# Layer 1 of a two-layer cross-attention model: the DMA transposes issued by ScalarE instead of SyncE, and VectorE's reciprocals ahead of the scaling of x

## The chip, the cores and the metric

The kernel runs on one core of a Trainium2 chip. The metric is the device time in microseconds (us) of one execution. The time before is the median of three runs, 813.28 us.

## The reference, cut to what matters

Two layers work on x of 32 blocks (batches) of 128 rows by 128 columns. Layer 0 is a cross-attention of 16 heads of 8 columns and a routed feed-forward block of 8 experts. The change touches only layer 1, for each block:

```python
def _act_quant(x):
    scale = 127.0 / jnp.clip(jnp.max(jnp.abs(x), axis=-1, keepdims=True), 1e-05)
    xq = jnp.clip(jnp.round(x * scale), -128.0, 127.0) / scale

# attention of layer 1: 16 heads of 64 columns, one null key and value beside the 128 of the context
sim = jnp.einsum('bhid,bhjd->bhij', q * scale, k)
attn = jax.nn.softmax(sim, axis=-1)
out = jnp.einsum('bhij,bhjd->bhid', attn, v)
out = _ln(out @ Wo, lno_s, lno_b)

# feed-forward of layer 1, with weights rounded to -1, 0, 1 and activations rounded to 8 bits
gate = jax.nn.silu(_bitlinear(x, w_gate))
up = _bitlinear(x, w_up)
return _bitlinear(gate * up, w_down)
```

## The kernel before, in words

Every engine has an instruction list of its own, written out by hand, and the engines are held together by semaphores alone. An engine takes its list strictly in order, so an instruction that waits holds back all that stand behind it. This holds for the queues that issue DMAs too: SyncE's (SP) list consists of waits and DMA issues.

Layer 0 ends at about 345 us. Then the loop of layer 1 runs over b = 0 to 31, one pass for each block, in `attention_ffn_block`. In pass b the attention of block b is computed, while the queries, keys and first score product of block b + 1 are made ready, the output projection and norm of earlier blocks are finished, and the feed-forward part of block f = b - 3 is worked on. A pass of the loop stands in the lists of all engines:

- TensorE (`tensor_part`): scores of b, queries of b + 1 (L1807), values of b (L1849), keys of b + 1 (L1819), the gate product of f (`gate_part`, L1953), the down product of f - 1 (`down`, L1988), the up product of f (L1964), the weighted values of b (L1915), the sums of the exponentials (`sums`, L1926 and L1928), the output projection of b - 1 (L1834), and small products with the row maxima (L1892, L1902). `gate_part(f)` writes the bank `pb`, which held half of the values of block b, so it waits until ScalarE has copied those out: `pe.wait_ge(v_ready, 2 * (f + 3) + 1)`.
- ScalarE (`scalar_part`): exponentials of half a block (`exps`, L2090), copies of queries (L2115), of row maxima (L2094), of values (`v_copy`, L2120), the tanh (L2126), the second exponentials, more copies, the scaling of h (L2133), and as the last of a pass `maxima_copy(b + 1, 0)` (L2094).
- VectorE (`vector_part`): row maxima, norms, the product of the attention output with the reciprocals (`normalise`, L2252, twice), and at the end of a pass `multiply(f)` (L2317), `h_range(f)` (L2323 to L2328), `quantise_x(b - 2)` (six instructions, L2292 to L2305, that end in `xq`, the rounded x in bf16), and `inverse(b)` (L2243), the reciprocals `rT` of the sums.
- GpSimd (`pool_part`): gathers, small norms, and the rounding of h to `hq` (`hidden_round`, L1583).
- SyncE (`sync_part`): stores and loads, and two chains. The first spreads the reciprocals over the partitions through DRAM: `store_reciprocals(b)` (L1474, `a_r_rows<-a_rT`), which waits for `inverse(b)`, and then `spread(b)`, four DMAs (L1483, `a_r_all<-a_r_rows`), which wait for the landing of the first. `normalise(b)`, in VectorE's next pass, waits for them. The second chain turns `xq` and `hq` by DMA transposes: `turn_x(b - 2)` (L1462, `f_xqT<-f_xq`) and `turn_h(b - 3)` (L1467, `f_hqT<-f_hq`), whose results `gate_part` and `down` use in the next pass.

The order in SyncE's list is what ties these together:

```python
            if 2 <= b < LAST + 2:
                turn_x(b - 2)
            if b + 1 < B:
                store_reciprocals(b)
            if 3 <= b < H_LAST + 3:
                turn_h(b - 3)
            if b + 1 < B:
                spread(b)
```

Of the kernel before, what the change touches and what calls it, by code (L numbers as in the profile page):

```python
# [18 lines left out]
def wait(eng, sem, value):  # L19

    if isinstance(value, int) and value <= 0:
        return
    eng.wait_ge(sem, value)
# [1256 lines left out]
def attention_ffn_block(nc, ctx, consts, w, wff, early, x_res, psum, before, gathered, out):  # L1280
# [3 lines left out]
    B, S, D, F = 32, P, P, 512  # L1284
    FC = F // P
# [98 lines left out]
    LAST = B - 3  # L1384
# [6 lines left out]
    H_LAST = LAST - 1  # L1391
# [58 lines left out]
    def sync_part(sp):  # L1450
        def context(b):
            sp.wait_ge(xcn_ready, b - 1)
            sp.dma_start(cin[:, b % 2, :], w["ctx"][b]).then_inc(cin_ld[b % 2], 16)

        def store(f):
            sp.wait_ge(x4_ready, f + 1)
            sp.dma_start(out[f], x4[:, f % 2, :]).then_inc(stored[f % 2], 16)

        def turn_x(f):
            sp.wait_ge(xq_ready, f + 1)  # L1460
            wait(sp, up_done, f)
            sp.dma_start_transpose(xqT[:].unsqueeze(1), xq[:]).then_inc(xq_in, 16)  # L1462

        def turn_h(f):
            sp.wait_ge(hq_ready, f + 1)
            wait(sp, down_done, f)
            sp.dma_start_transpose(hqT[:].rearrange("p (c q) -> p c q", c=FC), hq[:]).then_inc(hq_in, 16)  # L1467

        def store_reciprocals(b):
            sp.wait_ge(inverse_seq, b + 1)  # L1470
            if b >= 1:
                for half in range(2):
                    sp.wait_ge(r_spread[half], 32 * b)
            sp.dma_start(r_rows, rT[0:P:G, :]).then_inc(r_stored, 16)  # L1474

        def spread(b):
            sp.wait_ge(r_stored, 16 * (b + 1))
            if b >= 1:
                sp.wait_ge(oT_ready, 2 * b)
            for half in range(2):  # L1480
                for e in range(2):
                    rows = r_rows.rearrange("(a e i) q -> a e (i q)", a=2, e=2)[half, e]
                    sp.dma_start(r_all[e * HD:(e + 1) * HD, half, :], rows.partition_broadcast(HD)).then_inc(r_spread[half], 16)  # L1483

        context(2)
        context(3)
        for b in range(B):
            if b >= 4:
                store(b - 4)
            if 1 <= b and b + 3 < B:  # L1490
                context(b + 3)
            if 2 <= b < LAST + 2:
                turn_x(b - 2)
            if b + 1 < B:
                store_reciprocals(b)
            if 3 <= b < H_LAST + 3:
                turn_h(b - 3)
            if b + 1 < B:
                spread(b)
        for f in range(B - 4, B):  # L1500
            store(f)
        for s in range(2):
            sp.wait_ge(stored[s], 16 * (B // 2))
# [562 lines left out]
    def scalar_part(act):  # L2066
        act.wait_ge(w_in, N_W)
        act.wait_ge(setup_done, 4)

        def xc_copy(b):  # L2070
            act.wait_ge(tr_done, b + 1)
            wait(act, q_done, 2 * (b - 1))
            nc.scalar.activation(xT[:, b % 2, :], xcp[b][:, 0:S], ACT.Identity, bias=b1[:], scale=s1[:]).then_inc(xT_ready, 1)  # L2073
            if b >= 2:
                wait(act, cTm_ready, b)
                nc.scalar.activation(cT[:], xcp[b][:, S:2 * S], ACT.Identity, bias=1.0, scale=1.0).then_inc(cT_ready, 1)

        def xq_copy(f):
            act.wait_ge(xqt_done, f - LAST + 1)
            wait(act, up_done, f)  # L2080
            nc.scalar.copy(xqT[:], xtp[f]).then_inc(xqT_ready, 1)

        def exps(b, half):
            act.wait_ge(t_done, 2 * b + half + 1)
            for e in range(2):
                if half == 0:
                    wait(act, sums_done, b)
                else:
                    wait(act, pv_done, 2 * b)
                nc.scalar.activation(pT[:, 2 * half + e, :], tp[e], ACT.Exp, scale=SCALE).then_inc(exp_ready, 1)  # L2090

        def maxima_copy(b, half):
            act.wait_ge(row_done, 2 * b + half + 1)
            nc.scalar.copy(mxT[:, half, :], (pb, maxp[1])[half][:, 2 * S:3 * S]).then_inc(row_ready, 1)  # L2094

        def reciprocal_copy(half):
            act.wait_ge(row_done, 2 * B + half + 1)
            if half == 0:
                act.wait_ge(oT_ready, 2 * (B - 1))
            nc.scalar.copy(r_all[:, half, :], r_bank[half]).then_inc(row_ready, 1)  # L2100

        def null_exp(b):
            act.wait_ge(row_ready, 2 * b + 2)
            wait(act, sums_done, b)
            nc.scalar.activation(pnT[:], mxT[:, 1, :], ACT.Exp, scale=SCALE).then_inc(pn_ready, 1)

        def k_copy(b):
            act.wait_ge(k_done, 2 * b + 2)
            wait(act, t_done, 2 * (b - 1))
            nc.scalar.copy(kT[:, b % 2, 4:8, :].rearrange("p n k -> p (n k)"), key_bank(b, 1)).then_inc(kT_ready[1], 1)  # L2110

        def q_copy(b, half):
            act.wait_ge(q_done, 2 * b + half + 1)
            wait(act, t_done, 2 * (b - 1))
            nc.scalar.copy(qT[:, b % 2, 4 * half:4 * half + 4, :].rearrange("p n q -> p (n q)"), (pa, pb)[half]).then_inc(qT_ready, 1)  # L2115

        def v_copy(b, half):
            act.wait_ge(v_done, 2 * b + half + 1)
            wait(act, pv_done, 2 * (b - 1))
            nc.scalar.copy(v[:, b % 2, 8 * half:8 * half + 8, :].rearrange("p h d -> p (h d)"), value_bank(b, half)).then_inc(v_ready, 1)  # L2120

        def gate_tanh(f):
            act.wait_ge(gate_done, f + 1)
            act.wait_ge(sg_ready, 2 * f + 2)
            wait(act, gt_ready, f)
            nc.scalar.activation(th[:], gate_of[f], ACT.Tanh, scale=sgh[:, f % 2:f % 2 + 1]).then_inc(th_ready, 1)  # L2126

        def h_scale(f):
            act.wait_ge(hr_ready, f + 1)
            if f == 0:  # L2130
                act.wait_ge(p_set, 3)
            wait(act, hq_ready, f)
            nc.scalar.activation(ht[:], h[:], ACT.Identity, scale=hr[:], bias=big_m[:]).then_inc(ht_ready, 1)  # L2133

        def h_copy(f):
            act.wait_ge(htr_done, f - H_LAST + 1)
            wait(act, down_done, f)
            nc.scalar.copy(hqT[:], htp[f]).then_inc(hqT_ready, 1)

        for b in range(2):  # L2140
            v_copy(b, 0)
            v_copy(b, 1)
        xc_copy(0)
        q_copy(0, 0)
        q_copy(0, 1)
        maxima_copy(0, 0)
        for b in range(B):
            more = b + 1 < B
            f = b - 3 if b >= 3 else None
            if b == 0:  # L2150
                xc_copy(1)
            exps(b, 0)
            if more:
                q_copy(b + 1, 0)
            maxima_copy(b, 1)
            if b >= 2:
                v_copy(b, 0)
            if f is not None:
                gate_tanh(f)
            null_exp(b)  # L2160
            exps(b, 1)
            if b >= 2:
                v_copy(b, 1)
            if more:
                q_copy(b + 1, 1)
            if f is not None:
                h_scale(f)
            if b >= 1 and more:
                k_copy(b + 1)
            if b + 2 < B:  # L2170
                xc_copy(b + 2)
            if not more:
                break
            maxima_copy(b + 1, 0)
        f = LAST
        xq_copy(f)
        reciprocal_copy(0)
        reciprocal_copy(1)
        h_copy(f - 1)
        gate_tanh(f)  # L2180
        xq_copy(f + 1)
        gate_tanh(f + 1)
        h_scale(f)
        xq_copy(f + 2)
        gate_tanh(f + 2)
        h_copy(f)
        h_scale(f + 1)
        h_scale(f + 2)
        h_copy(f + 1)
        h_copy(f + 2)  # L2190

    def vector_part(dve):
# [46 lines left out]
        def inverse(b):  # L2239
            dve.wait_ge(sums_done, b + 1)  # L2240
            if b >= 1:
                dve.wait_ge(r_stored, 16 * b)
            nc.vector.reciprocal(rT[:], denP).then_inc(inverse_seq, 1)  # L2243
# [107 lines left out]
        for b in range(B):  # L2351
# [22 lines left out]
            if f is not None:  # L2374
                multiply(f)
                h_range(f)
            if b >= 2:
                quantise_x(b - 2)
            inverse(b)
            if b < 3:  # L2380
                weight_signs(b)
        f = LAST
# [147 lines left out]
```

## Time and profile before

| | us |
|---|---|
| median of three runs | 813.28 |
| lowest and highest | 813.21, 814.16 |
| the profiled execution, its own time | 821.97 |
| its span, first to last instruction | 820.2 |
| busy in the span: TensorE matmul | 775.9 (95%) |
| VectorE | 661.5 (81%) |
| GpSimd | 479.6 (58%) |
| ScalarE | 436.1 (53%) |

The granted TensorE clock is 0.975 of full speed over the span, and 1.00 in every stretch of layer 1 from 360 to 800 us. A busy share is the time in which at least one instruction of the engine ran, as a share of the span. Issuing a DMA isn't counted as busy; the profile lists such issues under SPq for SyncE's queue and ACTq for ScalarE's. Weight loads of TensorE stand apart as PEld and overlap the matmuls.

### The profile page before, as it was taken

The numbers are of one execution on the slowest core, as the hardware profiler recorded it, in microseconds if no ns is written. First come the engines' busy times: TensorE is split into PE (matmuls) and PEld (weight loads), VectorE is DVE, ScalarE is ACT, GpSimd is POOL, SyncE is SP. The second block draws the span as 40 slices with busy tenths as digits, with TensorE's granted clock in tenths as the row PEclk, the third lists the DMA queues.
The fourth block names the chain that finished last, engine by engine and source line by source line (L and its number), as shares of the span: only waits on it lengthen the run. The fifth ranks groups of instructions, "written<-read, shape, count | busy, mean of one in ns | idle before, by whom it ended". The sixth has DMA issues, their size and how long they took to land.

```text
span 820.2 us, 28896 instructions
## 1 busy us (share of the span) xinstructions
PE 775.9 (95%) x10878; PEld 655.3 (80%) x10908; DVE 661.5 (81%) x1747; ACT 436.1 (53%) x1049; POOL 479.6 (58%) x912
## 2 busy tenths in 40 slices
PE   8999999998898997999999999999999999999983
PEld 6777777776698996888888888888888888888861
DVE  6888989877756664578889888888898888988876
ACT  4666666656065773445455554554554545545542
POOL 7767678887856773335554654654655646555234
PEclk9999999989999999999999999999999999999995
DMA  8986220000421211112132231231221222213110
GB/s 245 374 331 255 102 86 15 16 21 28 142 72 49 64 50 36 38 50 64 48 77 57 54 81 47 54 82 46 67 69 48 81 52 55 81 48 76 42 39 14
DMA packets 72892, 66.76 MB, mean 81 GB/s; under 512 B 28354, under 2 KB 53682, under 8 KB 72754
## 3 DMA queue, kind: packets, MB, share of 16 engines
q1 hardware_dynamic: 57890, 40.66, 18.0%
q10 hardware_dynamic: 12816, 20.06, 6.6%
q0 software_dynamic: 2048, 4.20, 1.7%
q8 instruction: 87, 1.43, 0.7%
q14 instruction: 51, 0.42, 0.2%
HBM read 35.89 MB, written 24.37 MB: 73 GB/s over the span
## 4 chain that ended last, share of the span: by engine, by line
PE 49%; DVE 22%; SPq 11%; DMA 10%; issue 5%; ACT 1%; POOL 1%; DVEq 1%; another core or an unknown queue 0%; POOLq 0%; ACTq 0%
DMA a_r_all<-a_r_rows 7%; SPq L1483 4%; PE psum L1039 4%; PE psum L432 4%; PE psum L421 3%; DVE a_mxf L2231 3%; PE psum L1027 3%; PE psum L414 3%; PE psum L1807 3%; SPq L1462 3%; PE psum L1915 3%; PE psum L1881 2%; SPq L1467 2%; PE psum L1834 2%; DVE f_h L2317 2%
## 5 line engine op out<-in xcount | busy, mean ns | idle before, releaser
L2090 ACT ACTIVATE a_pT<-psum 128x512 f32<-128x512 f32 x128 | 69.5, 594 | 63.4 <-PE psum L1902 41.1
L1589 POOL TENSOR_TENSOR f_hd<-f_hmc,a_wmean 128x1 f32<-128x1 f32 x32 | 6.8, 212 | 135.5 <-DVE f_hr L2328 134.3
L720 DVE TENSOR_REDUCE l_mx<-psum 128x4 bf16<-128x512 f32 x128 | 81.8, 681 | 4.5 <-PE psum L403 2.9
L2231 DVE TENSOR_REDUCE a_mxf<-psum 128x8 f32<-128x1024 f32 x64 | 77.5, 1210 | 5.3 <-PE psum L1871 5.3
L1807 PEld LDWEIGHTS psum<-a_xT,a_Wq 128*128 128x128 f32 x512 | 66.5, 197 | 18.2 <-issue 14.1
L1819 PEld LDWEIGHTS psum<-a_cTm,a_Wk 128*128 128x128 f32 x512 | 64.3, 192 | 13.9 <-issue 13.9
L552 ACT ACTIVATE l_pT<-psum 128x512 f32<-128x512 f32 x128 | 70.6, 597 | 8.5 <-PE psum L421 8.2
L1807 PE MATMUL psum<-a_xT,a_Wq 128*128 128x128 f32 x512 | 73.2, 288 | 0.6 <-ACT a_xT L2073 0.6
L1583 POOL TENSOR_SCALAR f_hq<-f_ht 128x512 bf16<-128x512 f32 x31 | 60.4, 1947 | 19.9 <-ACT f_ht L2133 19.8
L1881 PE MATMUL psum<-a_qT,a_kT 64*128 64x128 f32 x1024 | 71.5, 280 | 0.0
L1849 PE MATMUL psum<-a_Wv,a_cTm 128*128 128x512 f32 x128 | 69.7, 630 | 0.0
L1819 PE MATMUL psum<-a_cTm,a_Wk 128*128 128x128 f32 x512 | 67.1, 275 | 0.0
L2133 ACT ACTIVATE f_ht<-f_h,f_big_m,f_hr 128x512 f32<-128x512 f32 x32 | 26.0, 814 | 72.2 <-DVE f_hr L2328 70.0
L1915 PE MATMUL psum<-a_pT,a_v 128*32 128x128 f32 x2048 | 63.0, 274 | 0.3 <-DVE a_oT L2252 0.3
L1881 PEld LDWEIGHTS psum<-a_qT,a_kT 64*128 64x128 f32 x1024 | 62.5, 189 | 0.0
L1834 PE MATMUL psum<-a_Wo,a_oT 128*128 128x128 f32 x512 | 62.5, 275 | 0.0
L1915 PEld LDWEIGHTS psum<-a_pT,a_v 128*32 128x32 f32 x2048 | 53.7, 110 | 9.0 <-issue 7.0
L1834 PEld LDWEIGHTS psum<-a_Wo,a_oT 128*128 128x128 f32 x512 | 59.7, 192 | 0.0
L421 PEld LDWEIGHTS psum<-negI,l_mx 128*128 128x128 bf16 x512 | 35.3, 100 | 25.6 <-DVE l_mx L720 22.7
L2252 DVE TENSOR_TENSOR a_oT<-psum,a_r_all 128x512 f32<-128x512 f32 x64 | 41.9, 680 | 9.1 <-issue 5.9
L1100 ACT ACTIVATE e_hT<-psum,e_w1t 128x128 f32<-128x128 f32 x156 | 44.6, 369 | 6.5 <-issue 5.9
L2120 ACT COPY a_v<-psum 128x512 f32<-128x512 f32 x64 | 37.6, 587 | 18.7 <-PE psum L1849 18.7
(315 smaller groups left out, 2075.4 us busy)
## 6 DMA issues: line engine op xcount, KB each, us to landing
sorted_x<-r_zeros ACTq DMA_DIRECT2D x12, 1408.0 KB, 6.9
a_r_all<-a_r_rows SPq DMA_DIRECT2D x124, 128.0 KB
e_xt<-sorted_x SPq DMA_DIRECT2D x39, 64.0 KB, 1.8
sorted_y<-e_yt ACTq DMA_DIRECT2D x39, 64.0 KB, 1.6
e_w<-in_E_W1b SPq DMA_DIRECT2D x1, 2064.0 KB
a_cin<-in_ctx SPq DMA_DIRECT2D x32, 64.0 KB, 2.5
out<-f_x SPq DMA_DIRECT2D x32, 64.0 KB, 2.2
x_res<-in_x SPq DMA_DIRECT2D x1, 512.0 KB, 5.6
```

The lines of the kernel that those rows point to most:

```text
L421: last = nc.tensor.matmul(tp[k][:, j * S:(j + 1) * S], mx[:, b % 2, h:h + 1].to_broadcast([P, P]), negI[:], start=False, stop=(j == Q4 - 1 ...
L552: nc.scalar.activation(pT[:, k, :], tp[k], ACT.Exp, scale=SCALE).then_inc(exp_ready, 1)
L720: nc.vector.tensor_reduce(mx[:, s, Q4 * k:Q4 * k + Q4], maxp[k % 2].rearrange("p (h t) -> p h t", h=Q4), AX_X, ALU.max).then_inc(mx_ready, 1)
L1583: nc.gpsimd.tensor_scalar(hq[:], ht[:], -M, 127.0, ALU.add, ALU.min).then_inc(hq_ready, 1)
L1807: last = nc.tensor.matmul(bank[:, i * S:(i + 1) * S], Wq[:, 4 * half + i, :], xT[:, b % 2, :], start=True, stop=True)
L1819: last = nc.tensor.matmul(bank[:, i * S:(i + 1) * S], Wk[:, 4 * half + i, :], cTm[:, b % 2, :], start=True, stop=True)
L1834: last = nc.tensor.matmul(pa[:, 0:D], oT[:, p, :], Wo[:, p, :], start=(p == 0), stop=(p == NP - 1))
L1849: nc.tensor.matmul(bank, cTm[:, b % 2, :], Wv[:, 512 * half:512 * half + 512], start=True, stop=True).then_inc(v_done, 1)
L1881: last = nc.tensor.matmul(tp[e][:, i * S:(i + 1) * S], kT[r, b % 2, p, :], qT[r, b % 2, p, :], start=(half == 0 and i == 0), stop=(half == ...
L1915: last = nc.tensor.matmul(op[half][32 * j:32 * j + 32, i * S:(i + 1) * S], v[:, b % 2, 8 * half + 4 * e + i, part], pT[:, 2 * half + e, i ...
L2090: nc.scalar.activation(pT[:, 2 * half + e, :], tp[e], ACT.Exp, scale=SCALE).then_inc(exp_ready, 1)
L2231: nc.vector.tensor_reduce(mxf[:, 8 * half:8 * half + 8].rearrange("p (e h) -> p e h", e=2), psum[:, 0:2, :].rearrange("p e (h t) -> p e h ...
```

## The change

`turn_x` and `turn_h` move from SyncE's list into ScalarE's, with the same waits and the same DMAs. In ScalarE's pass they stand at the end, behind `maxima_copy(b + 1, 0)` and ahead of the next pass's `exps(b + 1, 0)`. In VectorE's pass `inverse(b)` moves ahead of `quantise_x(b - 2)`. Nothing is added or taken away.

```diff
@@ sync_part
-        def turn_x(f):
-            sp.wait_ge(xq_ready, f + 1)
-            wait(sp, up_done, f)
-            sp.dma_start_transpose(xqT[:].unsqueeze(1), xq[:]).then_inc(xq_in, 16)
-
-        def turn_h(f):
-            sp.wait_ge(hq_ready, f + 1)
-            wait(sp, down_done, f)
-            sp.dma_start_transpose(hqT[:].rearrange("p (c q) -> p c q", c=FC), hq[:]).then_inc(hq_in, 16)
...
-            if 2 <= b < LAST + 2:
-                turn_x(b - 2)
             if b + 1 < B:
                 store_reciprocals(b)
-            if 3 <= b < H_LAST + 3:
-                turn_h(b - 3)
-            if b + 1 < B:
                 spread(b)
@@ scalar_part
+        def turn_x(f):
+            act.wait_ge(xq_ready, f + 1)
+            wait(act, up_done, f)
+            act.dma_start_transpose(xqT[:].unsqueeze(1), xq[:]).then_inc(xq_in, 16)
+
+        def turn_h(f):
+            act.wait_ge(hq_ready, f + 1)
+            wait(act, down_done, f)
+            act.dma_start_transpose(hqT[:].rearrange("p (c q) -> p c q", c=FC), hq[:]).then_inc(hq_in, 16)
...
             maxima_copy(b + 1, 0)
+            if b >= 2:
+                turn_x(b - 2)
+            if f is not None:
+                turn_h(f)
@@ vector_part
                 multiply(f)
                 h_range(f)
+            inverse(b)
             if b >= 2:
                 quantise_x(b - 2)
-            inverse(b)
```

ScalarE's list from the scaling of h (`f_ht`) at the end of one pass to the copy of the values (`a_v`) in the next. Before:

```order
L2133 ACTIVATE f_ht<-f_h,f_big_m,f_hr 128x512
L2110 COPY a_kT<-psum 128x512
L2073 ACTIVATE a_xT<-psum,a_b,a_s 128x128
L2076 ACTIVATE a_cT<-psum 128x128
L2094 CAST a_mxT<-psum 128x128
L2090 ACTIVATE a_pT<-psum 128x512 x2
L2115 COPY a_qT<-psum 128x512
L2094 CAST a_mxT<-psum 128x128
L2120 COPY a_v<-psum 128x512
```

and with the change:

```order
L2128 ACTIVATE f_ht<-f_h,f_big_m,f_hr 128x512
L2105 COPY a_kT<-psum 128x512
L2058 ACTIVATE a_xT<-psum,a_b,a_s 128x128
L2061 ACTIVATE a_cT<-psum 128x128
L2089 CAST a_mxT<-psum 128x128
L2071 DMA_TRANSPOSE f_xqT<-f_xq 128x1x128
L2076 DMA_TRANSPOSE f_hqT<-f_hq 128x4x128
L2085 ACTIVATE a_pT<-psum 128x512 x2
L2110 COPY a_qT<-psum 128x512
L2089 CAST a_mxT<-psum 128x128
L2115 COPY a_v<-psum 128x512
```

The two transposes now stand between the copy of the row maxima (`a_mxT`) and the exponentials (`a_pT`).

VectorE's list at the end of a pass, from the reciprocal of h's range (`f_hr`) to the copy of the output projection (`a_o`). Before:

```order
L2328 RECIPROCAL f_hr<-f_hmc 128x1
L2292 TENSOR_SCALAR f_xn<-x_res,a_ag,f_rs 128x128
L2294 TENSOR_REDUCE f_am<-f_xn 128x1
L2297 TENSOR_SCALAR f_amc<-f_am 128x1
L2299 RECIPROCAL f_rc<-f_amc 128x1
L2301 TENSOR_SCALAR f_xt<-f_xn,f_rc 128x128
L2305 TENSOR_SCALAR f_xq<-f_xt 128x128
L2243 RECIPROCAL a_rT<-psum 128x128
L2258 TENSOR_TENSOR a_o<-psum,a_null_out 128x128
```

and with the change:

```order
L2327 RECIPROCAL f_hr<-f_hmc 128x1
L2242 RECIPROCAL a_rT<-psum 128x128
L2291 TENSOR_SCALAR f_xn<-x_res,a_ag,f_rs 128x128
L2293 TENSOR_REDUCE f_am<-f_xn 128x1
L2296 TENSOR_SCALAR f_amc<-f_am 128x1
L2298 RECIPROCAL f_rc<-f_amc 128x1
L2300 TENSOR_SCALAR f_xt<-f_xn,f_rc 128x128
L2304 TENSOR_SCALAR f_xq<-f_xt 128x128
L2257 TENSOR_TENSOR a_o<-psum,a_null_out 128x128
```

The reciprocals `a_rT` have moved ahead of the six instructions that make `f_xq`.

## Rows read from the trace of the kernel before

**Rows 1.** Busy time by stretch: length, then each engine's busy us (instructions), clock, DMA.
```profile
core 0: us, PE busy (x) PEld busy (x) DVE busy (x) ACT busy (x) POOL busy (x), PEclk, DMA share, GB/s
617.91:632.61 14.70, 14.61 (x225) 12.68 (x225) 13.08 (x36) 7.73 (x17) 8.02 (x17) 1.00 0.23 64
632.61:647.31 14.70, 14.61 (x225) 12.68 (x226) 12.93 (x36) 7.73 (x17) 8.01 (x17) 1.00 0.22 64
647.31:662.05 14.74, 14.65 (x226) 12.72 (x226) 13.06 (x35) 7.77 (x17) 8.01 (x17) 1.00 0.22 62
543.07:559.00 15.93, 15.47 (x229) 12.94 (x229) 13.16 (x35) 7.68 (x17) 8.04 (x17) 1.00 0.24 59
...
379.40:779.80 400.40, 395.74 (x6017) 341.88 (x6043) 352.50 (x913) 208.70 (x432) 210.76 (x425) 1.00 0.24 62
```
**Rows 2.** Waits from 380 to 780 us: total, times, longest.
```profile
PEld psum L1871 <- DVE a_rT L2243: 2.2, 5, 0.6
DVE a_oT L2252 <- DMA a_r_all<-a_r_rows: 1.4, 3, 0.7
PEld psum L1915 <- DVE a_oT L2252: 1.4, 4, 0.6
```
**Rows 3.** Timeline of SyncE's queue in the pass from 543.07 us: start, us.
```profile
545.05 2.20 SPq L1467 DMA_TRANSPOSE f_hqT<-f_hq  x1
547.93 3.03 SPq L1483 DMA_DIRECT2D a_r_all<-a_r_rows  x4
```
**Rows 4.** Timeline of VectorE around the end of the pass at 632.61 us.
```profile
630.64 0.16 DVE L2328 RECIPROCAL f_hr<-f_hmc 128x1 f32<-128x1 f32 x1
630.72 0.33 DVE L2292 TENSOR_SCALAR f_xn<-x_res,a_ag,f_rs 128x128 f32<-128x128 f32 x1
...
632.46 0.23 DVE L2305 TENSOR_SCALAR f_xq<-f_xt 128x128 bf16<-128x128 f32 x1
632.61 0.95 DVE L2243 RECIPROCAL a_rT<-psum 128x128 f32<-128x128 f32 x1
634.42 0.29 DVE L2258 TENSOR_TENSOR a_o<-psum,a_null_out 128x128 f32<-128x128 f32 x1 [0.87 <-PE psum L1834]
...
641.04 1.27 DVE L2252 TENSOR_TENSOR a_oT<-psum,a_r_all 128x512 f32<-128x512 f32 x2
```
**Rows 5.** Timeline of TensorE, matmuls and two weight loads (PEld), same pass.
```profile
631.00 0.49 PE L1928 MATMUL psum<-a_pnT,a_null_rows 128*128 128x128 f32 x2
634.22 0.22 PE L1892 MATMUL psum<-negI,a_mx 128*128 128x128 bf16 x1
...
637.85 0.86 PEld L1819 LDWEIGHTS psum<-a_cTm,a_Wk 128*128 128x128 f32 x7 [0.24 <-issue]
638.74 0.10 PEld L1953 LDWEIGHTS psum<-f_wq,f_xqT 128*128 128x128 bf16 x1
```
**Rows 6.** Timeline of SyncE's queue, same pass.
```profile
632.72 1.11 SPq L1462 DMA_TRANSPOSE f_xqT<-f_xq  x1
633.93 0.52 SPq L1474 DMA_DIRECT2D a_r_rows<-a_rT  x1
634.55 1.24 SPq L1467 DMA_TRANSPOSE f_hqT<-f_hq  x1
635.88 2.47 SPq L1483 DMA_DIRECT2D a_r_all<-a_r_rows  x4
639.91 0.36 SPq L1457 DMA_DIRECT2D out<-f_x  x1
```
**Rows 7.** One source line, L1474: the issues of the store of the reciprocals.
```profile
L1474 SPq DMA_DIRECT2D a_r_rows<-a_rT x31: 492/522/585, 339.5 to 781.1; - x31
...
DMA to landing us min/median/max: 1.7/1.7/3.5
```
**Rows 8.** Chain of waits, same pass: the last spread DMA, start and us.
```profile
637.75 2.81 DMA a_r_all<-a_r_rows
```
**Rows 9.** Timeline of ScalarE, same pass, idle time before in brackets.
```profile
634.48 0.27 ACT L2094 CAST a_mxT<-psum 128x128 bf16<-128x128 f32 x1 [0.95 <-PE psum L1892]
635.99 1.09 ACT L2090 ACTIVATE a_pT<-psum 128x512 f32<-128x512 f32 x2 [1.25 <-PE psum L1902]
637.07 0.59 ACT L2115 COPY a_qT<-psum 128x512 f32<-128x512 f32 x1
637.56 0.27 ACT L2094 CAST a_mxT<-psum 128x128 bf16<-128x128 f32 x1
638.04 0.59 ACT L2120 COPY a_v<-psum 128x512 f32<-128x512 f32 x1 [0.22 <-PE psum L1849]
```
**Rows 10.** One source line, L1467 and then L1462: issues (min/median/max ns) and landing.
```profile
L1467 SPq DMA_TRANSPOSE f_hqT<-f_hq x28: 1232/1237/2314, 381.3 to 781.8; - x28
...
DMA to landing us min/median/max: 2.5/2.5/4.3
...
L1462 SPq DMA_TRANSPOSE f_xqT<-f_xq x29: 1107/1118/1816, 362.3 to 779.9; - x29
...
DMA to landing us min/median/max: 2.3/2.3/4.3
```
**Rows 11.** Timeline of ScalarE in layer 0, a DMA issue between two of its instructions.
```profile
251.75 0.27 ACT L1089 COPY e_xtT<-psum 128x128 f32<-128x128 f32 x1 [0.99 <-PE psum L1019]
251.76 0.33 ACTq L1093 DMA_DIRECT2D sorted_y<-e_yt  x1
252.19 1.14 ACT L1100 ACTIVATE e_hT<-psum,e_w1t 128x128 f32<-128x128 f32 x4 [0.17 <-issue]
```
**Rows 12.** Timeline of GpSimd, the rounding of h, same pass.
```profile
631.74 1.95 POOL L1583 TENSOR_SCALAR f_hq<-f_ht 128x512 bf16<-128x512 f32 x1 [0.65 <-ACT f_ht L2133]
```

## The prediction
> **What bounds the kernel now.** I read the page first, then the busy time by stretch, the waits of layer 1, and last the timelines of one pass on all engines. The page names DMAs and SyncE's queue in the chain that ended last, and it is tempting to read the change from that. The stretches say something else. A pass of the loop, counted from one `a_rT` to the next, takes 14.70, 14.70 and 14.74 us where nothing disturbs it, a mean of 14.71, and TensorE is busy for all but 0.09 us of each [rows 1]. So TensorE sets the pass, and whatever does not stop TensorE is free. Some passes are longer: the one from 543.07 us takes 15.93 us [rows 1]. The 27 passes from 379.4 to 779.8 us take 400.40 us, and 27 x 14.71 is 397.2, so disturbed passes cost 3.2 us in all. The waits name their cause: TensorE waits for `a_rT`, or for `a_oT`, whose writer waits for the DMAs of the reciprocals [rows 2]. In the pass from 543.07 us the issue of `turn_h` took 2.20 us, and the four spread DMAs behind it in SyncE's list started late [rows 3]. That 3.2 us is all that a faster chain of reciprocals can give.
>
> **VectorE's new order.** It moves one instruction ahead of six and adds none. The reciprocals need the sums, whose last matmul ends at 631.00 + 0.49 = 631.49 us [rows 5], while `f_hr` ends at 630.80 [rows 4]. So VectorE will wait some 0.7 us, start `a_rT` at about 631.5 and end it at 632.5, where it ended at 633.56. `f_xn` starts 0.08 us before the end of what stands ahead of it, and from its start to the end of `f_xq` is 632.69 - 630.72 = 1.97 us [rows 4], so `f_xq` ends at 634.4 instead of 632.7. Behind it stands `a_o`, which TensorE lets start at 634.42 anyway [rows 4]; the 0.87 us of idle time there covers the new wait, with nothing to spare. Cost: nothing. The bounds are nothing and some 0.3 us a pass if the sums are signalled later than their row says.
>
> **SyncE's list.** It loses two issues a pass. The store of `a_rT` can go at 632.5 instead of 633.93 us [rows 6]; it lands 1.7 us after its issue [rows 7], at 634.3, and the four spreads go then, not at 635.88 behind `turn_h` [rows 6]. The last of them was in flight until 637.75 + 2.81 = 640.56 [rows 8], with 0.5 us to spare before `a_oT` at 641.04 [rows 4]. That grows to about 2 us, more than the lateness of a disturbed pass. Gain: the 3.2 us. Bounds: nothing, if the disturbances move to other DMAs, and 3.2.
>
> **ScalarE's list.** Here is the price. ScalarE is busy only 7.73 of 14.70 us [rows 1], but the place matters. Before, the copy of the maxima starts at 634.48, then ScalarE waits for TensorE until the exponentials at 635.99, and goes on back to back: queries, maxima, and the copy of the values, which starts at 638.04 after 0.22 us of idle time and ends at 638.63 [rows 9]. The gate product needs that copy, because it writes the same bank; its weights are loaded at 638.74, and the load before it ended at 638.71 [rows 5]. So TensorE finds the bank free just in time: there is 0.1 us of slack.
>
> Now two issues stand between. On SyncE's queue they take 1.12 and 1.24 us, in the median [rows 10], and 0.10 us passes between one issue and the next, 633.93 - (632.72 + 1.11) [rows 6]. The trace has no transpose issued by ScalarE. What it has is a plain DMA issued by it in layer 0: the issue starts beside the running copy and takes 0.33 us, and the next activation starts 0.10 us behind the end of the issue, at 252.19, with 0.17 us of idle time that no other engine explains [rows 11]. So an issue does hold up ScalarE's next instruction. Their length I bound by 0.33 us each [rows 11] from below and by 1.82 and 2.31 us, the longest of each on SyncE [rows 10], from above, and take SyncE's medians, the same instruction on the nearest queue. Both inputs are there: `f_xq` at 634.4 as above, `f_hq` at 631.74 + 1.95 = 633.69 us [rows 12]. `turn_x` is issued from 634.55 to 635.67, `turn_h` from 635.77 to 637.01, and the exponentials start at 637.11, 1.12 us late. The 0.21 us before the copy of the values takes up a part: it ends at 634.48 + 2.63 + (637.56 + 0.27 - 635.99) + 0.59 = 639.54. The gate's weights load at 639.57 instead of 638.74: TensorE stalls 0.83 us. The landings are no matter: `turn_h` lands 2.5 us after its issue [rows 10], at 638.3.
>
> Does anything give the 0.83 us back? No: TensorE has no idle time in a pass, everything behind the gate moves along with it, and the next copy of maxima waits for TensorE again [rows 9]. There are 28 passes with both issues [rows 10]; the one with `turn_x` alone ends its issue at 635.7, ahead of the exponentials. So 28 x 0.83 = 23.2 us.
>
> A long issue used to hurt only when it exceeded the spare 0.5 us of the spread; on ScalarE every excess goes to TensorE. I put 1.9 us for all of them: two are in rows 3 and 10, about 1 us over the median each; bounds 0 and 4.
>
> A rule of the Trainium skill speaks to the price. DMA: Bandwidth & Descriptors, section Issuing engines are not separate DMA queues, says that starting DMAs on several engines saves only the sequencer's time to start them, which is usually small against the DMA itself. Here the row shows 1.12 of 2.3 us, not small, and the trace disagrees in that; by the rule the stall would be nothing and the sum -3.2 us, the first rival below.
>
> **The sum.** 23.2 + 1.9 - 3.2 = +21.9 us. The profiled execution's span of 820.2 us would be 842.1, its own time 843.9. It stands 8.7 us above the median of the runs, 813.28, which would be 835.2 us. About 0.2%, 1.6 us, is what a measurement of this kernel can tell from no change.
>
> **The rivals.**
> (1) Faster. The issues hold ScalarE for little. The point from which it decides: from the start of the maxima's copy at 634.48 to the exponentials at 635.99 are 1.51 us, and 0.21 and 0.1 us more are taken up, so two issues with their gaps that take under 1.8 us stall nothing. With 0.33 us each as in rows 11 they would take about 0.9. Then only the gain is left: 813.3 - 3.2 = 810.1 us. For it: ScalarE's only issues in the trace are that short, and rows 9 show idle time just there. Against it: the transposes' issue on SyncE is three times as long, and a queue's name does not shorten it. 11%.
> (2) The same. The two take about 1.9 us, the stall is 0.11 us and pays back the gain: 813 us. 4%.
> (3) Much slower. Transposes issued by ScalarE run beside the spreads issued by SyncE, which now start at the same time, 634.3 to 634.6 us. If that stretches each issue to the longest of rows 10, 1.82 + 2.31 instead of 2.36 us, a pass loses 1.77 us more, 28 x 2.60 - 3.2 = +70: 883 us. For it: long issues exist. Against it: rows 6 show the two kinds in flight together already, `turn_h` at 634.55 and the spreads from 635.88, with median lengths. Some of it, up to about 860, is as likely as all. 13%.
> That the change does not do what it says can be left out: the lists above show both moves.
>
> **How the numbers follow.** The forecast, 835.2 us, has 72%. Its own range: issues a fifth shorter, 28 x 0.5 = 14 us less, would give 821; VectorE's 0.3 us in all passes, 8 us, and all 4 us of long issues give 845. I take 824 as the lower end and reach up to 862 into the third rival, of which half lies below; rival 1 and 2 and the rest of rival 3 are left out. Faster than before by over 0.2%: rival 1, 11%. Within 0.2%: 4%. Slower: 85%.
>
> **What the profile after would show.** Right: passes of about 15.5 us without much scatter; a wait of about 0.8 us on TensorE ahead of the gate product, ended by the copy of the values; `f_xq` about 1.7 us later against TensorE's sums, and `a_rT` about 1.1 us earlier; the spreads issued from about 1.6 us earlier, and no wait of `a_oT` for their DMA. The two issues on ScalarE's queue at 1.1 and 1.2 us, and the exponentials 0.1 us behind them. Wrong: exponentials that start while an issue still runs, issues that are far from these lengths, or TensorE waiting first at another place than the gate.

## The result, and the profile after

| | before | changed |
|---|---|---|
| median of 4 runs, us | 813.25 | 869.88 |
| lowest and highest | 812.69, 814.16 | 863.21, 873.61 |
| profiled execution, its own time / span | 821.97 / 820.2 | 869.89 / 868.1 |
| 27 passes of layer 1, mean of one | 14.83 | 16.45 |

The medians differ by 56.6 us, a quotient of 1.0696. The measured ratio is 1.0672, with a 95% interval of 1.0636 to 1.0708, by which it would be 54.7 us. The forecast was 835.2 us, the range ended at 862. The direction was right and the size was not.

The waits of the changed kernel from 380 to 820 us (who waited for what: total, times, longest) show ScalarE's exponentials waiting for the two issues, and two places where TensorE stands:

```profile
ACT a_pT L2085 <- issue: 70.9, 27, 3.6
...
PE psum L1973 <- DMA f_hqT<-f_hq: 42.4, 26, 3.0
...
PEld psum L1973 <- DMA f_hqT<-f_hq: 17.9, 26, 1.6
...
PEld psum L1938 <- issue: 16.6, 16, 2.0
...
PEld psum L1938 <- DMA f_xqT<-f_xq: 11.9, 11, 1.8
```

L1938 is the gate product, where I expected the only stall. L1973 is `down`, which needs the result of `turn_h`. PE and PEld rows of one line are the same standstill seen twice, and the matmul records of L1938 are missing, so the idle time of PE at L1973 includes the gate's and is no measure of the second place. The weight loads keep them apart: 16.6 + 11.9 = 28.5 us ahead of the gate, 11.9 of it until `turn_x` landed, and 17.9 us ahead of `down` until `turn_h` landed. No row of `a_oT` waiting for the spread DMAs is left among the waits; before there was one [rows 2].

The source lines of the two transposes (issue min/median/max ns; landing min/median/max us):

```profile
L2071 ACTq DMA_TRANSPOSE f_xqT<-f_xq x29: 1112/1126/1923, 365.0 to 824.1; - x29
...
  PEld psum L1938: 23.3, 17
...
DMA to landing us min/median/max: 3.7/4.2/6.0
...
L2076 ACTq DMA_TRANSPOSE f_hqT<-f_hq x28: 1222/1232/2345, 381.5 to 826.0; - x28
...
  PE psum L1973: 45.5, 27
```

The issues take on ScalarE's queue what they took on SyncE's, 1.13 and 1.23 us in the median [rows 10]. The landing does not: 4.2 us for `turn_x` instead of 2.3. For `turn_h` the page gives none; by the last update of its semaphore in each pass, read from the trace, the median is 4.46 us instead of 2.48.

One of the faster passes, on ScalarE (the timeline, start and us):

```profile
645.55 0.27 ACT L2089 CAST a_mxT<-psum 128x128 bf16<-128x128 f32 x1 [0.95 <-PE psum L1877]
645.61 1.12 ACTq L2071 DMA_TRANSPOSE f_xqT<-f_xq  x1
646.83 1.23 ACTq L2076 DMA_TRANSPOSE f_hqT<-f_hq  x1
648.16 1.09 ACT L2085 ACTIVATE a_pT<-psum 128x512 f32<-128x512 f32 x2 [2.35 <-issue]
649.13 0.59 ACT L2110 COPY a_qT<-psum 128x512 f32<-128x512 f32 x1
649.60 0.30 ACT L2089 CAST a_mxT<-psum 128x128 bf16<-128x128 f32 x1
649.76 0.63 ACT L2115 COPY a_v<-psum 128x512 f32<-128x512 f32 x1
```

The exponentials start 648.16 - 645.61 = 2.55 us behind the start of the first issue; the prediction had 2.56. On SyncE's queue and on TensorE in that pass:

```profile
645.28 2.43 SPq L1473 DMA_DIRECT2D a_r_all<-a_r_rows  x4
...
650.50 0.10 PEld L1938 LDWEIGHTS psum<-f_wq,f_xqT 128*128 128x128 bf16 x1 [0.72 <-issue]
...
651.02 0.40 PE L1973 MATMUL psum<-f_wq,f_hqT 128*128 128x128 bf16 x4 [1.04 <-DMA f_hqT<-f_hq]
```

The gate's weights come 0.11 us behind the end of the copy of the values (650.39), with 0.72 us of idle time ahead of them: the stall that was forecast. Then TensorE waits again for `f_hqT`. And the spreads begin at 645.28, ahead of both transposes, where they used to begin 1.33 us behind the start of `turn_h` [rows 6]. The stretches (as in rows 1) show that a fast pass costs 15.69 us, with TensorE's busy time as before, and that in some passes the clock falls as well:

```profile
642.60:658.29 15.69, 14.64 (x225) 12.63 (x225) 12.76 (x34) 7.60 (x17) 7.96 (x16) 1.00 0.23 60
...
409.06:418.00 8.94, 7.37 (x78) 6.42 (x76) 7.01 (x22) 3.60 (x9) 6.76 (x14) 1.00 0.58 74
418.00:421.00 3.00, 1.61 (x18) 1.51 (x21) 0.97 (x3) 0.88 (x2) 1.03 (x2) 0.62 0.14 41
421.00:424.00 3.00, 3.00 (x24) 2.23 (x21) 2.79 (x5) 1.08 (x2) 0.00 (x0) 0.50 0.15 44
```

### The profile page after: what moved, and what is told of

It reads as the page before. It is cut to its first block, busy times and chain, and to the rows that moved or that the text cites. A ratio compares the mean times of both kernels' runs of the same rounds, so it can differ in the third digit from the quotient of the medians.

```text
span 868.1 us, 28896 instructions
## 1 busy us (share of the span) xinstructions
PE 781.9 (90%) x10878; PEld 658.3 (76%) x10908; DVE 651.9 (75%) x1747; ACT 430.7 (50%) x1049; POOL 478.9 (55%) x912
## 3 DMA queue, kind: packets, MB, share of 16 engines
q0 software_dynamic: 2048, 4.20, 1.7%
## 4 chain that ended last, share of the span: by engine, by line
PE 69%; DMA 15%; DVE 5%; ACTq 5%; issue 3%; POOL 1%; ACT 1%; DVEq 0%; POOLq 0%
DMA f_hqT<-f_hq 14%; PE psum L1900 7%; PE psum L1819 6%; PE psum L1792 4%; PE psum L1834 4%; PE psum L1866 4%; ACTq L2071 4%; PE psum L432 4%; PE psum L1039 4%; PE psum L421 3%; PE psum L1804 3%; PE psum L414 3%; PE psum L1911 3%; PE psum L1027 3%; PE psum L403 2%
## 5 line engine op out<-in xcount | busy, mean ns | idle before, releaser
L1866 PE MATMUL psum<-a_qT,a_kT 64*128 64x128 f32 x1024 | 73.5, 285 | 0.0
L1834 PE MATMUL psum<-a_Wv,a_cTm 128*128 128x512 f32 x128 | 71.8, 647 | 0.0
L1568 POOL TENSOR_SCALAR f_hq<-f_ht 128x512 bf16<-128x512 f32 x31 | 60.4, 1947 | 20.6 <-ACT f_ht L2128 20.5
L1866 PEld LDWEIGHTS psum<-a_qT,a_kT 64*128 64x128 f32 x1024 | 64.3, 193 | 0.0
L2242 DVE RECIPROCAL a_rT<-psum 128x128 f32<-128x128 f32 x32 | 30.6, 957 | 36.6 <-PE psum L1913 36.6
L1973 PE MATMUL psum<-f_wq,f_hqT 128*128 128x128 bf16 x128 | 13.7, 234 | 49.3 <-DMA f_hqT<-f_hq 45.5
```

The lines of the kernel that those rows point to most:

```text
L1568: nc.gpsimd.tensor_scalar(hq[:], ht[:], -M, 127.0, ALU.add, ALU.min).then_inc(hq_ready, 1)
L1834: nc.tensor.matmul(bank, cTm[:, b % 2, :], Wv[:, 512 * half:512 * half + 512], start=True, stop=True).then_inc(v_done, 1)
L1866: last = nc.tensor.matmul(tp[e][:, i * S:(i + 1) * S], kT[r, b % 2, p, :], qT[r, b % 2, p, :], start=(half == 0 and i == 0), stop=(half == ...
```

## The experiments

Theory A: the transposes land late because they share the DMA engines with the spreads, which the change lets start ahead of them. Theory B: a transpose issued by ScalarE is slow in itself. Beside these stands the question what the two issues cost ScalarE.

**queue_only**: VectorE's order as before, the rest as changed.

```diff
-            inverse(b)
             if b >= 2:
                 quantise_x(b - 2)
+            inverse(b)
```

> The transposes on ScalarE's queue, VectorE's order as before. Theory A (contention): the transposes land late because the four spread DMAs, 512 KB a pass, are started ahead of them and run on the same DMA engines. Here the reciprocals come at their old time, so the spreads start about 0.7 us behind turn_x instead of 0.3 us ahead of it, and turn_h 0.4 us behind them instead of 1.5 us: turn_x lands in about 2.3 to 3 us, turn_h in 3 to 4, and the time is 835 to 855 us, below the changed kernel's 870. Theory B (queue): a transpose issued by ScalarE is slow in itself, 3.8 to 4.5 us, whatever the spreads do: the time stays at 865 to 875 us.

Measured: 868.48 us against 815.10 for the kernel before on that chip, ratio 1.0661 (1.0623 to 1.0699). `turn_x` landed in 4.0 us, `turn_h` in 4.5. That is theory B's number, and A as I had put it fell: 0.48 us of a head start (the median) is not enough for `turn_x`. The new order on VectorE is no part of the loss here; with the transposes on ScalarE's queue it changes nothing that these runs can tell.

**after_small_spreads** and **before_small_spreads**: the changed kernel and the one before, with

```diff
-                    sp.dma_start(r_all[e * HD:(e + 1) * HD, half, :], rows.partition_broadcast(HD)).then_inc(r_spread[half], 16)
+                    sp.dma_start(r_all[e * HD:(e + 1) * HD, half, 0:16], rows[0:16].partition_broadcast(HD)).then_inc(r_spread[half], 16)
```

and `r_all` set to 1.0 once before the loop. Both kernels leave the attention's scaling out for the other 496 of the 512 columns.

> The changed kernel with the four spread DMAs cut to 16 of 512 columns each (same count, same partitions, 1/32 of the bytes; the other reciprocals are left at 1.0, so the attention's scaling is left out for them). Theory A: the transposes land in 2.3 and 2.5 us; TensorE is left with the wait for the copy of the values alone, 0.53 us in 28 passes, against a kernel without disturbances at 810: 825 us. Theory B: landings of 3.8 to 4.5 us and 860 to 870 us.

> The kernel before with the same cut of the spread DMAs: the control for the run above. Both theories: the disturbed passes go, every pass 14.7 us, 810 us (813 if the disturbances are not the spreads' own). The difference of the two runs is what two issues on ScalarE's queue cost by themselves: 28 x 0.53 = 15 us by the stall seen at the gate product, 28 x 0.83 = 23 us by my prediction.

Measured: 845.33 us for the changed kernel, 813.78 for the one before; their ratios to the kernel before are 1.0351 (1.0307 to 1.0394) and 0.9980 (0.9964 to 0.9996). With 1/32 of the spreads' bytes the same transposes on the same queue land earlier; the two source lines of after_small_spreads:

```profile
L2072 ACTq DMA_TRANSPOSE f_xqT<-f_xq x29: 1112/1126/1833, 361.9 to 800.5; - x29
...
DMA to landing us min/median/max: 2.7/2.7/4.6
...
L2077 ACTq DMA_TRANSPOSE f_hqT<-f_hq x28: 1222/1234/2197, 378.4 to 802.3; - x28
...
DMA to landing us min/median/max: 2.8/3.0/4.3
```

So B falls: the queue is the same, the landing is not. A's figures were missed as well: it had landings of 2.3 and 2.5 us and a time of 825 us, where 1/32 of the bytes still gave 2.7 and 3.0 us, and 845 us. The bytes of the spreads are worth 869.9 - 845.3 = 24.6 us in the changed kernel, by the medians, and 1.3 us in the one before. What is left, 845.3 - 813.8 = 31.5 us, is the hold on ScalarE with the clock's share in it, and at most 2.1 us of waits for the transposes in the stretch from 380 to 780 us; it is more than either of my two figures. Two passes of after_small_spreads by stretch (columns as in rows 1), and below them ScalarE's timeline in the second:

```profile
436.78:452.20 15.42, 14.86 (x226) 12.72 (x225) 13.06 (x35) 7.54 (x17) 8.00 (x16) 1.00 0.12 27
405.05:421.37 16.32, 14.86 (x226) 12.71 (x225) 12.94 (x35) 7.63 (x17) 7.99 (x16) 1.00 0.12 26
```

```profile
408.07 1.15 ACTq L2072 DMA_TRANSPOSE f_xqT<-f_xq  x1
409.31 2.11 ACTq L2077 DMA_TRANSPOSE f_hqT<-f_hq  x1
411.52 1.08 ACT L2086 ACTIVATE a_pT<-psum 128x512 f32<-128x512 f32 x2 [3.25 <-issue]
```

An undisturbed pass takes 15.42 us, 0.71 over 14.71; 28 x 0.71 = 19.9 us. The other 11.6 us lie in passes like the one from 405.05 us, where a long issue adds its whole excess (2.11 - 1.23 = 0.88 us, and the pass is 0.90 us longer), and in the last pass, in which the trace has the granted clock at half for 10 us. By the trace it is 7.2 us in the 27 passes of the loop over 15.42 us each, and 4.6 us in the last pass, which took 19.26 us where the kernel before took 13.97.

**spreads_behind** and **spreads_after_issue**: the changed kernel with the spreads' start held back, in `spread(b)`:

```diff
             sp.wait_ge(r_stored, 16 * (b + 1))
+            if b >= 3:
+                sp.wait_ge(hq_in, 16 * (b - 2))
```

> The changed kernel, but SyncE starts the four spread DMAs of a pass only when turn_h of that pass has landed. Theory A: the transposes land in 2.3 and 2.5 us and TensorE no longer waits for f_hqT; the wait moves to a_oT, whose reciprocals now land 4.9 us after about 638.3 on the old pass's clock, 1 us too late: 840 to 860 us. Theory B: the transposes still take 3.8 to 4.5 us, the spreads start 1.8 us later still, and the time is 885 us or more.

```diff
             sp.wait_ge(r_stored, 16 * (b + 1))
+            sp.wait_ge(exp_ready, 4 * b + 5)
```

> The changed kernel, but the spreads start only when ScalarE has issued both transposes (SyncE waits for the exponential behind them), not when turn_h has landed. Theory A, contention of transfers in flight: a transpose that is issued in full before the spreads lands almost as if alone, 2.3 and 2.5 to 3 us, as on SyncE's queue before, and the reciprocals come 0.6 us earlier than in spreads_behind: 845 to 854 us, faster than the changed kernel's 870. If every spread within the transfer's flight counts, turn_h lands in 3.5 us or more and the time is above 854.

Measured: 854.06 us, ratio 1.0483 (1.0447 to 1.0519), and 843.53 us, 1.0375 (1.0329 to 1.0422). Both are faster than the changed kernel although they only add a wait; the second came 1.5 us below the range that I had written down. In spreads_after_issue all bytes are moved, and the two source lines read

```profile
L2072 ACTq DMA_TRANSPOSE f_xqT<-f_xq x29: 1112/1126/1979, 362.8 to 802.0; - x29
...
DMA to landing us min/median/max: 2.3/2.3/3.9
...
L2077 ACTq DMA_TRANSPOSE f_hqT<-f_hq x28: 1230/1232/2079, 379.3 to 803.7; - x28
...
DMA to landing us min/median/max: 2.4/2.5/3.4
```

as on SyncE's queue before [rows 10]. No wait for `f_hqT` is left. In spreads_behind the wait moved to `a_oT` (19.7 us in 19 waits), as A said.

**order_only**: the kernel before with `inverse(b)` ahead of `quantise_x(b - 2)`, everything else on its old queue.

> The kernel before with VectorE's new order alone; the transposes stay on SyncE's queue. f_xq is ready 1.7 us later, turn_x and the store of the reciprocals behind it go 1.7 us later, the spreads start at about 637.6 on the old pass's clock, and the second half lands 4.9 us on, 0.85 us after a_oT wants it. Both theories: transposes land in 2.3 and 2.5 us, TensorE waits for a_oT, 0.4 to 0.85 us in 28 passes: 825 to 840 us. A time at 813 would say that the reciprocals' chain has more slack than rows show.

Measured: 831.00 us, ratio 1.0199 (1.0160 to 1.0238). Its waits from 380 to 780 us:

```profile
DVE a_oT L2252 <- DMA a_r_all<-a_r_rows: 24.9, 24, 2.3
```

VectorE's order alone is a loss of 1.6 to 2.4%, because SyncE issues `turn_x` ahead of the reciprocals and the former now comes later. On SyncE's queue as its list stands, the order does not pay.

**turn_x_earlier**, and **turn_x_earlier_again**, the same kernel: both transposes on ScalarE's queue, VectorE's order as before.

```diff
+            if b >= 2:
+                turn_x(b - 2)
             maxima_copy(b + 1, 0)
-            if b >= 2:
-                turn_x(b - 2)
             if f is not None:
                 turn_h(f)
@@ spread(b)
             sp.wait_ge(r_stored, 16 * (b + 1))
+            sp.wait_ge(t_done, 2 * b + 3)
```

> Both transposes on ScalarE's queue, VectorE's order as before, turn_x moved ahead of the copy of the maxima into ScalarE's idle 0.95 us, turn_h behind that copy, and the spreads held until TensorE has the scores of the next block (635.95 on the old clock, about when they started before). If what ScalarE costs is its place in the list and not the queue, both issues fit into idle time: the exponentials are at most 0.1 us late, the transposes land in 2.3 and 2.5 to 3 us, and only long issues (about 1 us in a quarter of the passes) are left: 813 to 825 us. If ScalarE's queue costs in itself: 845 us or more.

> The kernel of turn_x_earlier once more, for a narrower interval. Its passes of layer 1 took 14.71 us in the mean where the kernel before takes 14.83, 3.2 us over 27 passes, while layer 0, which both have alike, ended at times that lay up to 7 us apart between executions. If the gain in the loop is real, the ratio is 0.996 to 0.999, and the profiled loop is again at 14.7 to 14.75 us a pass; if it was chance, 1.000 and more.

Measured: 815.08 us, ratio 1.0006 (0.9985 to 1.0027), and 815.32 us, ratio 1.0011 (0.9992 to 1.0030). Against queue_only, which differs by the place of one issue and the hold on the spreads, that is 53 us. ScalarE's timeline in one pass:

```profile
631.33 0.27 ACT L2090 CAST a_mxT<-psum 128x128 bf16<-128x128 f32 x1 [0.95 <-PE psum L1878]
631.39 1.23 ACTq L2077 DMA_TRANSPOSE f_hqT<-f_hq  x1
632.84 1.09 ACT L2086 ACTIVATE a_pT<-psum 128x512 f32<-128x512 f32 x2 [1.25 <-PE psum L1888]
```

`turn_h` ends at 632.62, before the exponentials may start, and these wait for TensorE again, not for the issue. The profiled loops ran at 14.71 and 14.72 us a pass, the gain of 3.2 us that I had foreseen, but the runs do not show it. It would be a ratio of 0.996, and the intervals begin at 0.9985 and 0.9992, so of the whole time at most 0.15% can have been gained, 1.2 us. What I had written down for the second run, 0.996 to 0.999 if the gain is real and 1.000 and more if it was chance, came out as chance. The kernel before has one traced execution against these two, which decides nothing of this size. Layer 0 is alike in all these kernels, and the first `a_rT` of the loop still came between 330.8 us in one trace and 338.5 us in another.

**no_hold**: turn_x_earlier without the line in `spread(b)`.

> turn_x_earlier without the hold on the spreads: they start as soon as the reciprocals have landed in DRAM, about 0.6 us behind the start of turn_h's issue on the other queue, where before and in turn_x_earlier they started 1.3 to 1.5 us behind it. Theory A (contention with whatever starts before the transpose's issue is complete): turn_h lands in 3.5 to 4.3 us instead of 2.5, TensorE waits for f_hqT, and the time is 818 to 828 us. If the hold is not needed, the time is turn_x_earlier's, 812 to 815 us, and turn_h lands in 2.5 us.

Measured: 815.16 us, ratio 1.0015 (0.9993 to 1.0036). The source line of `turn_h`:

```profile
L2076 ACTq DMA_TRANSPOSE f_hqT<-f_hq x28: 1227/1234/1934, 375.0 to 773.9; - x28
...
  PEld psum L1973: 2.1, 5
...
DMA to landing us min/median/max: 2.5/3.8/4.9
```

The landing is what A said, 3.8 us. The time is not: `turn_h` is issued early enough there for `down` to bear it, and TensorE waits in 5 passes alone, 2.1 us in all. A late landing costs only what exceeds the slack. And no_hold differs from queue_only by the place of `turn_x`'s issue alone, behind the maxima's copy there and ahead of it here: 868.5 against 815.2 us.

**merged**: the kernel before, with one spread DMA for each half.

```diff
-                for e in range(2):
-                    rows = r_rows.rearrange("(a e i) q -> a e (i q)", a=2, e=2)[half, e]
-                    sp.dma_start(r_all[e * HD:(e + 1) * HD, half, :], rows.partition_broadcast(HD)).then_inc(r_spread[half], 16)
+                rows = r_rows.rearrange("(a e i) q -> a e (i q)", a=2, e=2)[half]
+                sp.dma_start(r_all[:, half, :], rows.unsqueeze(1).broadcast_to([2, HD, Q4 * S])).then_inc(r_spread[half], 16)
```

> The kernel before with the four spread DMAs as two of 128 partitions, the same bytes. If the issues on SyncE's queue (2.47 us for four) make the reciprocals late in disturbed passes, the second half lands 0.6 us or more earlier, the waits for a_oT go, and the time is 810 to 813 us, up to 3 us below before. If the bytes set the landing, nothing changes: 813 to 815 us. If one DMA of 128 partitions is issued no faster than two of 64 and its first half lands later, up to 820.

Measured: 1046.2 us, ratio 1.2837 (1.2791 to 1.2884), outside everything that I had written down. The source line of the spreads:

```profile
L1482 SPq DMA_DIRECT2D a_r_all<-a_r_rows x62: 495/504/652, 338.2 to 1002.7; - x62
```

and the wait that followed:

```profile
PEld psum L1914 <- DVE a_oT L2251: 101.8, 34, 5.2
```

The issue is as short as hoped, 0.50 us for 256 KB, and the landing far too late. The Trainium skill (DMA: Bandwidth & Descriptors, section Why a DMA increments its semaphore by 16 and not by 1) says that a DMA is split over as many engines, up to 16, as divide the slowest dimension of both patterns; the source's is now 2. The trace agrees: from 380 to 780 us, two of the spreads' packets of 2048 bytes are in flight at once for 86% of the time in which there are any, never more than three but for under 1% of it, where the kernel before has mostly six to twelve, and one packet takes 84 ns in the median in both. Two at 84 ns make 49 GB/s; the slices that hold the spreads alone show about 50, where the four DMAs before move about 200.

Set side by side, the transposes' landings (medians of the 28 passes that have both, from the semaphores' updates) follow the distance to the start of the first spread DMA's issue, whichever queue issues them:

| | turn_h starts against the first spread, us | turn_h lands | turn_x starts | turn_x lands |
|---|---|---|---|---|
| spreads_behind | 2.5 ahead | 2.47 | 3.7 ahead | 2.29 |
| spreads_after_issue | 2.0 ahead | 2.47 | 3.2 ahead | 2.30 |
| turn_x_earlier | 1.5 ahead | 2.47 | 3.3 ahead | 2.29 |
| before | 1.3 ahead | 2.48 | 3.2 ahead | 2.27 |
| no_hold | 0.8 ahead | 3.79 | 2.6 ahead | 2.29 |
| queue_only | 0.7 behind | 4.54 | 0.5 ahead | 4.03 |
| changed | 1.6 behind | 4.46 | 0.3 behind | 4.21 |
| after_small_spreads | 1.6 behind | 3.03 | 0.3 behind | 2.77 |

The issue of `turn_h` takes 1.23 us. In the medians, where the spreads of full size began only after it, the landing was untouched; where they began within it or before it, it grew by 1.3 to 2 us. So theory A holds, but its condition is not the end of the issue. The single passes of no_hold and the packets in the traces put it closer. Only the two transposes move packets of 256 bytes (`turn_h` 512 of them); in the kernel before the last of these ends 2.00 us behind the start of `turn_h`'s issue, and the first packet of the spreads moves 1.34 us behind the start of theirs, 1.26 us in no_hold (medians). In three passes of no_hold the spreads were issued 0.95 to 0.98 us behind the start of `turn_h`, within its issue, and it landed in 2.47 us all the same. Of the passes of no_hold with an issue of usual length and bytes on time (in most of these kernels the bytes themselves are late in some passes, for reasons that no run looked for), the four in which the first spread packet moved 2.26 to 2.36 us behind the start of `turn_h` landed in 2.45 to 2.47 us, and the thirteen in which it moved at 2.13 us or before landed in 3.5 us or more. So in these traces a head start of about 1 us was enough: what counts is that the transpose's packets are through when the spreads' first one moves.

The packets show as well what is late. In no_hold the bytes of `turn_h` are through at 1.99 us in the median, as before, and only the landing behind them comes 1.3 us later. In the changed kernel the last of them ends at 2.98 us instead of 2.00, and the landing comes 1.48 us behind it instead of 0.48: half of the 2 us is in moving the bytes and half in what follows. What holds the landing up once the bytes are through stays open.

## Why the prediction was wrong, point by point

- **TensorE sets the pass**: right. It was busy 14.64 us in a pass of 15.69 as in one of 14.70, and the loss is what it stands still, with some at the lower clock.
- **VectorE's new order costs nothing**: right in the changed kernel. In that pass it waits for the sums as foreseen, and `f_xq` ended at 645.03, ahead of the maxima's copy. queue_only, without the new order, is no faster.

```profile
642.60 0.96 DVE L2242 RECIPROCAL a_rT<-psum 128x128 f32<-128x128 f32 x1 [0.80 <-PE psum L1913]
```

- **SyncE's gain of 3.2 us**: the waits for the spreads went. In the control, before_small_spreads, which has no such waits either, the profiled loop was 3.4 us shorter, 397.0 us in 27 passes, but the time only by 0.2% (0.9980, 0.9964 to 0.9996), 1.6 us. So at most a small gain, less than counted, and swamped here.
- **28 x 0.83 = 23.2 us on ScalarE**: the mechanism and its place were right, the exponentials 2.55 us behind the first issue and the gate waiting for the copy of the values. The stall is 0.71 us, since ScalarE's copies closed up a little more than I had them: 19.9 us. One reading in it was wrong: there was no slack of 0.1 us. In the kernel before and in the changed one alike the gate's weights load 0.11 us behind the end of the copy of the values, in the median of all passes, so the gate already waited for it. With 639.54 + 0.11 the stall would be 0.91 us; the copies take the 0.20 us off.
- **1.9 us for long issues**: mis-sized. In after_small_spreads this term and the clock make 11.6 us. I had taken two rows of the tail for the whole and bounded it by 4. In 27 passes of the changed kernel the two issues together exceed their medians, 2.36 us, by about 7 us, on SyncE before by about 3.5, and there the excess had 0.5 us of slack in each pass, on ScalarE none.
- **"The landings are no matter: `turn_h` lands 2.5 us after its issue, at 638.3"**: this is the step that failed, worth 24.6 us. The prediction put the landings at no cost. I carried over a landing that was measured with the spreads queued 1.33 us behind, into a schedule in which my own paragraph on SyncE had just moved them ahead. Measured, `turn_h` lands in 4.46 us: on the prediction's own clock at 635.77 + 4.46 = 640.23, behind the 638.87 + 0.83 = 639.70 at which `down` would load its weights, and `turn_x` in 4.2 us, for which the gate waited in 11 passes. The passes of about 15.5 us without much scatter, which were to show that I was right, came out at 15.6 to 20.5. I had both times, 634.3 for the spreads and 634.6 for the transposes, and set them side by side only in the third rival.
- **Rival 3** saw the right neighbours and priced the wrong thing: it let the contention lengthen the issues (they stayed at 1.13 and 1.23 us) instead of the landings. What I held against it, that the two kinds fly together before as well, was the misreading: there `turn_h` was issued in full at 635.79 and the first spread at 635.88 [rows 6], and by the packets the bytes of `turn_h` were through 0.7 us before the first of the spreads moved. The rows show two issues one behind the other, not two transfers at once.
- **Rival 1**, and beside it the rule of the Trainium skill (DMA: Bandwidth & Descriptors, section Issuing engines are not separate DMA queues) that the issue time is usually small against the DMA: for these issues it is not, 1.13 us where the landing took 2.3 us (spreads_after_issue). In turn_x_earlier, where the list leaves room for them, they cost nothing. The decisive figure, idle time where the issue stands, was right.
- **The clock** was in no term. In the pass from 409.06 us, TensorE has 2.96 us without a record ahead of `down`, the gate's product in it, until `f_hqT` landed, and then ran at a granted clock of 0.50, 1.2 GHz, for about 7 us; that pass took 20.48 us, some 2.8 us more than 14.71 and this gap. There were three such stretches in the changed kernel's loop, 17 us at half clock, and none in the loop before. Its four runs lie up to 10.4 us apart, with a mean granted clock of 0.983 in the fastest and 0.965 in the slowest; how much of that is these stretches is open, since 23 runs of the kernel before lie up to 7.6 us apart too.
- **The account.** The forecast had 21.9 us of the 56.6. Of the missing 34.7 the landings are 24.6, the long issues and the clock 11.6 - 1.9 = 9.7, the gain 3.2 - 1.3 = 1.9 by the control's median, and the smaller stall takes 3.3 off, 32.9 us together. The rest, 1.8 us, is the difference between the two sets of runs of the kernel before that these figures start from, 813.3 and 815.1 us.

## What to carry to other kernels

When a DMA is moved to another queue, write down for each transfer in flight what starts before it now and what used to start before it; a landing time measured behind one neighbour is no price beside another, and two queues lose the order that one queue gave for nothing. In this kernel a DMA issued by ScalarE, put ahead of work that it had ready, held it for the whole issue, so look for idle time at the exact place in its list, not for a low busy share: the same two issues cost some 30 us behind the copy of the maxima and nothing that could be measured with the first of them ahead of it. And a wait that is added to hold a bulk transfer back can pay: one line in SyncE's list took 26 us off the changed kernel (869.9 to 843.5).

## What was not expected of the hardware

The long DMA issues, 2.1 us instead of 1.24, coincide with the fetch of instructions. In the trace of the kernel before, of 18 issues between 380 and 790 us that exceed their line's median by over 0.25 us, 16 overlap a 16 KB packet on the queue q8; of the 230 others, 13 do. One of them, SyncE's timeline, and the DMA view of just that stretch, 664.00 to 666.05 us:

```profile
664.00 2.05 SPq L1467 DMA_TRANSPOSE f_hqT<-f_hq  x1
```

```profile
q8 instruction: 1, 0.02, 3.7%
issues: line engine op xcount, KB each, median us to landing
f_hqT<-f_hq SPq DMA_TRANSPOSE x1, 3.2
```

In the changed kernel it is 17 of 21, and 16 of the 202 others. No experiment took the fetches away, so this is a coincidence in time, not a cause shown.
